# Four states per input and scan instruction, a two-bank PSUM ring, and a reordered tile and prologue in a Mamba cross-attention block with a ternary FFN

## Chip, cores and metric

The kernel runs on one NeuronCore of one Trainium2 chip. The metric is device time of one execution in microseconds (us). A profiled execution gives the trace: the busy spans of TensorE (PE; PEld is its weight load), VectorE (DVE), ScalarE (ACT) and GpSimd (POOL), and the DMA traffic. SyncE (SP) only issues transfers. Each engine runs its own instructions strictly in order and waits on semaphores.

## What is computed

Input `x` is 4 x 512 x 512. A gated state-space (Mamba) block over the context is added to it, then a gated feed-forward net with ternary weights and 8-bit activations. Cut to what matters:

```python
x1    = in_proj_w @ ctx                       # 512 channels, 512 times
u     = silu(causal_conv4(x1) + conv_b)
dt_lo, Bm, Cm = split(x_proj_w @ u)           # 16, 16 and 16 rows
delta = softplus(dt_proj_w @ dt_lo + dt_proj_b)
# 16 states per channel, over time l:
state[l] = state[l-1] * exp(delta[l] * A) + (delta[l] * u[l]) * Bm[l]
y[l]     = sum_n state[l, n] * Cm[l, n]
x  = x + tanh(g_xattn) * (y + D * u) * silu(layernorm(x))
# FFN on rows of x, weights w1, w2, w3 ternarised by mean(|w|), rows quantised to 8 bits:
h  = silu(bitlinear(ln(x), w1, g1)) * bitlinear(ln(x), w2, g2)
x  = x + tanh(g_ffn) * bitlinear(h, w3, g3)
```

## The kernel before

The scan is cut into 16 tiles `k` (4 batches times 4 groups `et` of 128 channels) of 4 steps `q` each, so 64 steps `s = 4k + q`. In a step the 128 partitions hold 32 channels times 4 groups of states, and a partition runs 4 states one after the other along the free axis, 4 x 512 elements. One step is a pipeline over all engines:

- PE spreads `delta*u` of 32 channels over the partitions into the PSUM bank `du_ps` (`bcast_du(s)`, L1484). It waits until all input products of step s-1 have read the bank.
- ACT writes `dA`, the exponentials, four instructions a step (`exps(s)`, L874), two buffers.
- DVE multiplies `du_ps` by B into `dbu_ps` (`add_input(s, half)`, L1129) and scans (`scan(s, half)`, L1138) into `hb`. `dbu_ps` has two banks, so a step is two pairs of input and scan, two states each.
- POOL multiplies `hb` by C (`times_c(s)`, L668). For the last step of a tile with k >= 4 it does so in halves (L663), each of which waits for its own half of the scan.
- PE sums the states into `y_ps` (`sum_states(p)`, L1497, steps 2p and 2p+1 together).

Around the scan the same tile also carries the feed-forward net of earlier rows: row tile `f = k - 4` is normalised, quantised (`quant_scales`, `dequant_scales`) and multiplied by w1 and w2 (`gate_up`, eight PE jobs in step q = 3), and hidden tile `g = k - 5` goes through POOL products (`times_up` L632, `h_gain` L625), DVE maxima (`hidden_max` L1277), `hidden_rms` on POOL (L637, L639), `hidden_scales` on DVE (L1296 to L1298), `quant_hidden` on ACT, transposes and `down` on PE (L1606) and `output` on DVE (L1269). `gated_y(k-1)` (L1260) makes the gated output of the tile before; PE transposes it (`yzT`, L1580) and `add_scan(k-1)` (L1165) adds it to x1.

The order in each engine is written out by hand in one loop over k and q per engine. The relevant pieces: on DVE a step is `add_input(s,0)`, `scan(s,0)`, `add_input(s,1)`, then the tile's other work, `scan(s,1)`; in q = 1 that other work is the two `hidden_max`, `row_bias` and `gated_y`, and `hidden_scales` and `add_scan` come behind `scan(s,1)`. On POOL q = 0 is `times_c(4k-1)`, `times_up` twice, `row_rstd`, `h_gain` twice, and q = 1 is `times_c(4k)`, `hidden_rms`, `mul_du`, `mul_gains`, `hidden_deq`.

All other PE results (projections, convolutions, transposes, gate and up, down) go through a ring of four PSUM banks (`ring`, `NB = 4`). `ring_order()` writes down the order of all jobs; `take(job)` makes PE wait until the job NB places earlier has been read out (`freed_by`). `keep_clock` puts matmuls whose result is not used ahead of some jobs (`FILL`, L1569). When the scan ends (`TAIL`, rows 12 to 15 of the feed-forward net), only that net is left.

In the first 20 steps the weights pass twice through three buffers: ACT sums absolute values (L1034, `abs_chunks`), after step 6 DVE makes the scales (`weight_scales`, L1231), then from step 7 POOL makes one chunk a step ternary (L700), PE transposes it and ACT takes the sign (L1013). B and C of a batch are written to DRAM and read back spread over partitions (`store_bc`, `load_b`, `load_c`, L445 to L463) on SP's queue. `z_row_stats` (L1096) are the layer norm statistics of the gate.

## Times and profile before

| what | value |
|---|---|
| three runs | 718.72, 718.19, 714.82 us; median 718.19 |
| the profiled execution | 720.12 us, of which the span from first to last instruction is 718.1 us |
| DVE busy | 607.9 us (85%) |
| POOL busy | 548.3 us (76%) |
| ACT busy | 558.4 us (78%) |
| PE busy | 619.6 us (86%), in which matmuls of `keep_clock` count too |
| TensorE clock granted, mean | 0.909 |

The busy share of an engine is a mean over stages. The stages are: prologue to 40 us, tiles 0 to 4 with the weights (40 to 224 us), tiles 5 to 15 (224 to 639 us), tail (639 to 718 us). A timeline row gives the start, the time in us, engine, line, operation, output and inputs, and in brackets how long the engine sat idle before it and who ended that.

### The profile page before, as it was taken

The numbers are of one execution on the slowest core, as the hardware profiler recorded it, in microseconds if no ns is written. First come the engines' busy times: TensorE is split into PE (matmuls) and PEld (weight loads), VectorE is DVE, ScalarE is ACT, GpSimd is POOL, SyncE is SP. The second block draws the span as 40 slices with busy tenths as digits, with TensorE's granted clock in tenths as the row PEclk, the third lists the DMA queues.
The fourth block names the chain that finished last, engine by engine and source line by source line (L and its number), as shares of the span: only waits on it lengthen the run. The fifth ranks groups of instructions, "written<-read, shape, count | busy, mean of one in ns | idle before, by whom it ended". The sixth has DMA issues, their size and how long they took to land.

```text
span 718.1 us, 8217 instructions
## 1 busy us (share of the span) xinstructions
PE 619.6 (86%) x2538; PEld 248.4 (35%) x2538; DVE 607.9 (85%) x620; ACT 558.4 (78%) x805; POOL 548.3 (76%) x316
## 2 busy tenths in 40 slices
PE   6736765999869999999989999998897979796997
PEld 3311221544343333334333434332333323233443
DVE  2979959899967899987989899999999989877665
ACT  3647885689679997896879997989698969557873
POOL 2055549987598989897889999999899897967732
PEclk9865887999879999989999999999897979798999
DMA  8599873548922122233411212154111111000000
GB/s 220 168 257 330 287 269 91 165 148 231 297 86 74 44 59 74 59 81 83 93 28 53 52 47 56 46 120 102 49 55 45 45 44 45 15 16 0 16 31 29
DMA packets 40570, 72.01 MB, mean 100 GB/s; under 512 B 10912, under 2 KB 13472, under 8 KB 38352
## 3 DMA queue, kind: packets, MB, share of 16 engines
q1 hardware_dynamic: 37312, 62.07, 30.7%
q10 hardware_dynamic: 3216, 9.44, 3.9%
q8 instruction: 20, 0.33, 0.2%
q14 instruction: 22, 0.18, 0.1%
HBM read 50.51 MB, written 4.46 MB: 77 GB/s over the span
## 4 chain that ended last, share of the span: by engine, by line
PE 44%; DVE 17%; POOL 16%; issue 7%; DMA 7%; ACT 6%; SPq 2%; DVEq 0%; POOLq 0%; ACTq 0%
PE ring L1519 13%; DVE hb L1138 8%; PE y_ps L1497 7%; PE ring L1606 6%; POOL hb L668 6%; DVE dbu_ps L1129 5%; PE du_ps L1484 4%; POOL up_sb L625 4%; PE ring L1569 3%; POOL h L632 3%; DMA dl_rep<-delta 3%; DMA bc_rep<-bc_scratch 2%; PE ring L1446 2%; PE ring L1465 2%; PE ring L1456 2%
## 5 line engine op out<-in xcount | busy, mean ns | idle before, releaser
L1138 DVE TENSOR_TENSOR_SCAN hb<-dA,dbu_ps 128x1024 f32<-128x1024 f32 x128 | 292.4, 2284 | 13.5 <-ACT dA L874 4.6
L668 POOL TENSOR_TENSOR hb<-hb,bc_rep 128x2048 f32<-128x2048 f32 x52 | 235.8, 4537 | 46.7 <-DVE hb L1138 38.8
L874 ACT ACTIVATE dA<-dl_rep,a_neg 128x511 f32<-128x511 f32 x252 | 160.9, 714 | 18.9 <-DMA dl_rep<-delta 18.7
L1129 DVE TENSOR_TENSOR dbu_ps<-du_ps,bc_rep 128x1024 f32<-128x1024 f32 x128 | 157.6, 1231 | 18.5 <-PE du_ps L1484 8.2
L1497 PE MATMUL y_ps<-hb,sel_s 128*32 128x512 f32 x512 | 125.7, 636 | 2.2 <-POOL hb L668 2.2
L1484 PE MATMUL du_ps<-du,sel_q 32*128 32x512 f32 x128 | 79.9, 706 | 46.9 <-DVE dbu_ps L1129 46.5
L632 POOL TENSOR_TENSOR h<-h,up_sb 128x1024 f32<-128x1024 f32 x24 | 56.5, 2353 | 19.8 <-ACT up_sb L892 19.3
L1606 PE MATMUL ring<-w3T,hT 128*128 128x512 fp8e4 x256 | 61.5, 387 | 1.5 <-ACT hT L959 1.1
L663 POOL TENSOR_TENSOR hb<-hb,bc_rep 128x1024 f32<-128x1024 f32 x22 | 51.8, 2357 | 11.9 <-DVE hb L1138 11.6
L1497 PEld LDWEIGHTS y_ps<-hb,sel_s 128*32 128x32 f32 x512 | 28.5, 116 | 87.2 <-issue 81.5
L625 POOL TENSOR_TENSOR up_sb<-h,g3b 128x1024 f32<-128x1024 f32 x24 | 56.4, 2373 | 0.1
L1519 PE MATMUL ring<-w1T,a12T 128*128 128x512 fp8e4 x208 | 54.7, 386 | 1.9 <-ACT a12T L936 1.1
L1519 PE MATMUL ring<-w2T,a12T 128*128 128x512 fp8e4 x208 | 54.4, 384 | 0.0
L929 ACT ACTIVATE up_sb<-up_sb,h_sc 128x1024 f32<-128x1024 f32 x31 | 33.9, 1140 | 25.6 <-DVE h_sc L1298 25.6
L1569 PE MATMUL ring<-w1T,a12T 128*128 128x512 fp8e4 x178 | 48.6, 416 | 0.0
L1484 PEld LDWEIGHTS du_ps<-du,sel_q 32*128 32x128 f32 x128 | 20.5, 199 | 77.0 <-issue 76.5
L884 ACT ACTIVATE h<-ring,deq 128x512 f32<-128x512 f32 x48 | 32.7, 682 | 12.1 <-PE ring L1519 11.9
L1277 DVE TENSOR_REDUCE h_max<-up_sb 128x1 f32<-128x1024 f32 x32 | 38.1, 1210 | 1.8 <-POOL up_sb L625 1.8
L892 ACT ACTIVATE up_sb<-ring,deq 128x512 f32<-128x512 f32 x48 | 32.9, 685 | 7.3 <-PE ring L1519 7.3
L1465 PE MATMUL ring<-u,diag_w 128*128 128x512 f32 (+3 forms) x80 | 38.4, 626 | 0.0
L1446 PE MATMUL ring<-ctxT,w_inT 128*128 128x512 f32 x64 | 36.3, 708 | 2.3 <-ACT ctxT L779 2.3
L959 ACT ACTIVATE hT<-ring 128x1024 bf16<-128x1024 f16 x27 | 26.4, 1018 | 14.3 <-PE ring L1561 13.8
(174 smaller groups left out, 950.6 us busy)
## 6 DMA issues: line engine op xcount, KB each, us to landing
dl_rep<-delta SPq DMA_DIRECT2D x252, 64.0 KB, 2.0
bc_rep<-bc_scratch SPq DMA_DIRECT2D x32, 256.0 KB, 5.2
h<-in_L_ffn_w_dram SPq DMA_DIRECT2D x5, 1024.0 KB, 8.5
x<-in_L_ffn_w_dram SPq DMA_DIRECT2D x5, 1024.0 KB, 7.3
up_sb<-in_L_ffn_w_dram SPq DMA_DIRECT2D x5, 1024.0 KB, 7.9
xt<-in_x_dram SPq DMA_DIRECT2D x16, 256.0 KB, 3.1
out_dram<-x SPq DMA_DIRECT2D x16, 256.0 KB, 2.0
h<-in_L_ffn_w_dram ACTq DMA_DIRECT2D x3, 1024.0 KB, 6.1
```

Of the source, the lines that this page charges most:

```text
L625: g.tensor_tensor(gained(ft)[:, half], hidden(ft)[:, half], g3b[:, half], ALU.mult).then_inc(h_mul, 1)
L632: g.tensor_tensor(h[:, half], h[:, half], up_sb[:, half], ALU.mult).then_inc(h_pool, 1)
L668: g.tensor_tensor(hb[:, s % 4, :, :], hb[:, s % 4, :, :], c_rep(s // 16), ALU.mult)\
L874: ins = a.activation(dA[:, s % 2, i, 1:L], dl[:, 1:L], ACT.Exp, scale=a_neg[:, s % 16, i:i + 1])
L1129: v.tensor_tensor(dbu_ps[:, :, :], du_ps[:, :].unsqueeze(1).to_broadcast([P, 2, L]), b_rep(b)[:, 2 * half:2 * half + 2, :], ALU.mult).then ...
L1138: v.tensor_tensor_scan(hb[:, s % 4, 2 * half:2 * half + 2, :].rearrange("p a l -> p (a l)"), dA[:, s % 2, 2 * half:2 * half + 2, :].rearra ...
L1465: ins = mm(dst[:, shift:L], diag_w[:, DC - 1 - shift, :], u[:, m % UB, 0:L - shift], start=(shift == 0), stop=(shift == DC - 1))
L1484: mm(du_ps[:, :], sel_q[rows, :], du[rows, k % 2, :], start=True, stop=True).then_inc(du_bc, 1)
L1497: ins = mm(y_ps[32 * q:32 * q + 32, :], sel_s[:, :], hb[:, s % 4, i, :], start=False, stop=(i == NH - 1))
L1519: ins = mm(dst[:, :], rows_T(ft)[:, m, t, :], w[:, t, 512 * c:512 * (c + 1)], start=(t == 0), stop=(t == ET - 1))
L1569: mm(dst[:, :], rows_T(ft)[:, t % 2, t // 2 % ET, :], w1T[:, t % ET, 0:512], start=True, stop=True)
L1606: ins = mm(dst[:, :], hT[:, t, :], w3T[:, t, :], start=(t == 0), stop=(t == H // P - 1))
```

## The change

`dbu_ps` gets four banks, so one `add_input` and one `scan` do all four states of a step (2048 elements); only steps 0 and 63 stay in halves. The two banks come from the ring, which has `NB = 2` until the tail; from `TAIL_RING` on the four banks of `dbu_ps` are the ring (`TB = 4`). `times_c` is not changed: its halves now both find the whole scan.

On DVE `hidden_max`, `gated_y` and `hidden_scales` stand between input and scan of q = 1, `add_scan` and `quant_scales` between those of q = 2 (in tiles with et = 0 `add_scan` and the row statistics stay behind the scan of q = 1). `row_var` and `row_bias` of tiles with et other than 0 and `dequant_scales` go to POOL (`row_affine`, `dequant_scales`). POOL's q = 0 becomes `times_c`, `times_up` 0, `h_gain` 0, `times_up` 1, `row_affine`, `h_gain` 1, `hidden_rms`. Diagonal tap matrices are made once, four of them, at the start. Convolutions move from tiles with et = 3 to those with et = 0, which may have two. One `keep_clock` is left out in tiles with et 0 or 3.

In the prologue B of batch 0 is spread by four matmuls (`replicate_b`) and copied by DVE (`copy_b`), half of `z_row_stats` goes into steps 1 to 3, the tanh of the gates goes behind the third `silu_u`, the first three weight chunks are loaded ahead of `store_bc`, and later ones by ACT. The gain vector g3 is loaded in step 18 and not 15. Some small tiles share the buffer `hT` or `sel_q`.

```diff
-NB = 4
+NB = 2
+TB = 4
+def early_convs(k):
+    if k < LEARLY or k % ET == ET - 1:
+        return []
+    m = k + AHEAD - (k % ET == 0)
+    return [m] if m < KQ else []
+def late_convs(k):
+    if k < 1 or k % ET == ET - 1:
+        return []
+    if k % ET == 0:
+        m = [k + AHEAD] if k >= LEARLY else [k + AHEAD - 1, k + AHEAD]
+    else:
+        m = [k + AHEAD] if k < LEARLY else []
+    return [i for i in m if i < KQ]
-    first = (0, 0, 2, 4, 7, 10, WCH)
+    first = (0, 2, 4, 6, 8, 10, WCH)
-        dbu_ps = psum("dbu_ps", [P, 2, L])
+        dbu_ps = psum("dbu_ps", [P, NH, L])
...
+            def row_affine(ft):
+                if ft >= 4:
+                    pool.wait_ge(xn_done, ft - 3)
+                pool.wait_ge(row_square, row_sums(ft))
+                col = fsc[:, ft % 4, :]
+                link(g.tensor_scalar(col[:, 0:1], fmv[:, ft % 4, 1:2], (1.0 + RMS_EPS) / D, RMS_EPS * LN_EPS,
+                                     ALU.mult, ALU.add))
+                link(g.tensor_tensor(col[:, 1:2], col[:, 0:1], half_neg[:, :], ALU.pow))
+                g.tensor_tensor(col[:, 2:3], fmv[:, ft % 4, 0:1], col[:, 1:2], ALU.mult).then_inc(fbias, 1)
...
                     if q == 0 and gt >= 0:
                         times_up(gt, 0)
+                        h_gain(gt, 0)
                         times_up(gt, 1)
                         if f % ET:
-                            row_rstd(f)
-                        h_gain(gt, 0)
+                            row_affine(f)
                         h_gain(gt, 1)
-                    if q == 2 and k + 1 + AHEAD < KQ:
-                        diag_taps(k + 1 + AHEAD)
+                        hidden_rms(gt)
+                    if q == 2 and f >= 0:
+                        dequant_scales(f)
                     if q == 1:
-                        if gt >= 0:
-                            hidden_rms(gt)
...
-            def scan(s, half):
+            def scan(s, lo=0, hi=NH):
-                dve.wait_ge(exp_done, 2 * s + half + 1)
-                if half == 0 and s >= 4:
+                dve.wait_ge(exp_done, 2 * s + hi // 2)
+                if lo == 0 and s >= 4:
                     dve.wait_ge(sum_done, (s - 4) // 2 + 1)
...
-                                     ALU.mult, ALU.add).then_inc(scan_done, 1)
+                                     ALU.mult, ALU.add).then_inc(scan_done, (hi - lo) // 2)
...
-                    add_input(s, 0)
+                    ends = s in (0, Q * KQ - 1)
+                    if ends:
...
+                    else:
+                        add_input(s)
+                    if k == 0 and q >= 1:
+                        z_row_stats(KQ // 2 + 2 * q - 2)
+                        z_row_stats(KQ // 2 + 2 * q - 1)
...
                     if q == 1:
                         if k == 0:
                             convolve(AHEAD)
+                        if g >= 0:
+                            hidden_max(g, 0)
+                            top = hidden_max(g, 1)
+                        if k >= 1:
+                            gated_y(k - 1)
+                        if g >= 0:
+                            after(top)
+                            hidden_scales(g)
                     if q == 2:
                         if f >= 0 and f % ET == 0:
                             row_bias(f)
-                    scan(s, 0)
-                    add_input(s, 1)
+                        if k >= 1 and et:
+                            add_scan(k - 1)
+                        if f >= 0:
+                            quant_scales(f)
                     if q == 3 and g >= 0:
                         output(g)
...
-                    scan(s, 1)
+                    if ends:
+                        scan(s, 2, 4)
+                    else:
+                        scan(s)
                     if q == 1:
-                        if g >= 0:
-                            after(top)
-                            hidden_scales(g)
-                        if k >= 1:
+                        if k >= 1 and et == 0:
                             add_scan(k - 1)
...
+            def replicate_b(n):
+                dst, done = take(("brep", n))
+                mm(dst[:, :], sel_b()[0:DR + 2 * NS, P * n:P * (n + 1)], xdbl[:, :], start=True, stop=True).then_inc(done, 1)
```

## Rows read from the trace of the kernel before

**Rows 1.** Page: TensorE clock granted, in tenths, in 40 slices of the span.

```profile
PEclk9865887999879999989999999999897979798999
```

**Rows 2.** Instructions of line L1138: shortest, median, longest ns, first and last start.

```profile
L1138 DVE TENSOR_TENSOR_SCAN hb<-dA,dbu_ps x128: 2274/2286/2290, 41.6 to 636.8; 128x1024 f32<-128x1024 f32 x128
```

**Rows 3.** Windows: stretch, PE, PEld, DVE, ACT, POOL busy, clock, DMA.

```profile
437.40:473.80 36.40, 34.26 (x142) 12.31 (x141) 34.33 (x34) 34.23 (x50) 33.08 (x17) 0.97 0.19 53
```

**Rows 4.** Timeline of DVE, from the end of tile 10 into tile 11.

```profile
451.68 2.28 DVE L1138 TENSOR_TENSOR_SCAN hb<-dA,dbu_ps 128x1024 f32<-128x1024 f32 x1
454.06 1.23 DVE L1129 TENSOR_TENSOR dbu_ps<-du_ps,bc_rep 128x1024 f32<-128x1024 f32 x1
455.42 2.29 DVE L1138 TENSOR_TENSOR_SCAN hb<-dA,dbu_ps 128x1024 f32<-128x1024 f32 x1
...
461.47 1.23 DVE L1129 TENSOR_TENSOR dbu_ps<-du_ps,bc_rep 128x1024 f32<-128x1024 f32 x1
...
466.30 2.33 DVE L1277 TENSOR_REDUCE h_max<-up_sb 128x1 f32<-128x1024 f32 x2
...
468.67 0.68 DVE L1260 TENSOR_TENSOR yz<-y_ps,xt 128x512 f32<-128x512 f32 x1
469.27 2.28 DVE L1138 TENSOR_TENSOR_SCAN hb<-dA,dbu_ps 128x1024 f32<-128x1024 f32 x1
472.56 0.21 DVE L1296 TENSOR_SCALAR h_sc<-h_pow,h_max 128x1 f32<-128x1 f32 x1 [1.01 <-POOL h_pow L639]
...
473.14 0.73 DVE L1165 SCALAR_TENSOR_TENSOR x<-ring,gates,x 128x512 f32<-128x512 f32 x1
```

**Rows 5.** Timeline of POOL over the same stretch.

```profile
454.03 2.35 POOL L663 TENSOR_TENSOR hb<-hb,bc_rep 128x1024 f32<-128x1024 f32 x1 [1.03 <-DVE hb L1138]
456.34 2.35 POOL L632 TENSOR_TENSOR h<-h,up_sb 128x1024 f32<-128x1024 f32 x1
459.36 2.34 POOL L632 TENSOR_TENSOR h<-h,up_sb 128x1024 f32<-128x1024 f32 x1 [0.68 <-ACT up_sb L892]
461.66 0.55 POOL L653 TENSOR_TENSOR fsc<-fsc,half_neg 128x1 f32<-128x1 f32 x1
462.18 4.71 POOL L625 TENSOR_TENSOR up_sb<-h,g3b 128x1024 f32<-128x1024 f32 x2
466.86 4.51 POOL L668 TENSOR_TENSOR hb<-hb,bc_rep 128x2048 f32<-128x2048 f32 x1
471.36 0.29 POOL L637 TENSOR_SCALAR h_ss<-h_ss 128x1 f32<-128x1 f32 x1
471.73 0.72 POOL L639 TENSOR_TENSOR h_pow<-h_ss,halves 128x2 f32<-128x2 f32 x1
...
473.65 1.27 POOL L613 TENSOR_TENSOR a<-a,g1b 128x512 f32<-128x512 f32 x1
```

**Rows 6.** Timeline of DVE, prologue to tile 5: five rows of its waits.

```profile
33.12 2.46 DVE L1096 BATCH_NORM_STATS2 zst<-g3b 128x6 f32<-128x512 f32 x4
...
40.22 1.23 DVE L1129 TENSOR_TENSOR dbu_ps<-du_ps,bc_rep 128x1024 f32<-128x1024 f32 x1 [4.22 <-DMA bc_rep<-bc_scratch]
...
102.19 0.17 DVE L1231 TENSOR_REDUCE at<-wsum 128x3 f32<-128x12 f32 x1 [6.02 <-ACT up_sb L1034]
...
205.18 0.21 DVE L1189 TENSOR_SCALAR fsc<-fmv,fsc 128x1 f32<-128x1 f32 x1 [6.32 <-POOL fsc L653]
...
224.07 1.23 DVE L1129 TENSOR_TENSOR dbu_ps<-du_ps,bc_rep 128x1024 f32<-128x1024 f32 x1 [3.79 <-PE du_ps L1484]
```

**Rows 7.** Timeline of POOL in tile 4: its wait for C.

```profile
196.92 4.54 POOL L668 TENSOR_TENSOR hb<-hb,bc_rep 128x2048 f32<-128x2048 f32 x1 [7.93 <-DMA bc_rep<-bc_scratch]
```

**Rows 8.** Timelines of PE and ACT: a convolution, a two-tile softplus, a chunk load's issue.

```profile
429.18 3.69 PE L1465 MATMUL ring<-u,diag_w 128*128 128x512 f32 x8
```

```profile
130.18 0.43 ACTq L1017 DMA_DIRECT2D h<-in_L_ffn_w_dram  x1
...
316.19 1.41 ACT L856 ACTIVATE delta<-ring,dtb_col 128x512 f32<-128x512 f32 x2
```

More of the change, by code:

```diff
@@ L77, in ring_order @@
     jobs += [("inproj", m) for m in range(ET)] + [("xproj", 0), ("dt", 0), ("dt", 1)]
+    jobs += [("brep", n) for n in range(NH)]
     jobs += [("ctxT", 1, 0), ("ctxT", 1, 1), ("inproj", ET)]
@@ L236, in flamingo_block @@
         full = [sem(f"ring_full{j}") for j in range(NB)]
+        tail_full = [sem(f"tail_full{j}") for j in range(TB)]
         pool_seq = sem("pool_seq")
@@ L309, in bank, with filling @@
         def bank(job):
-            return ring[RING[job] % NB]
+            n = RING[job]
+            if n >= TAIL_RING:
+                return dbu_ps[:, (n - TAIL_RING) % TB, :]
+            return ring[n % NB]
+        def filling(job):
+            n = RING[job]
+            if n >= TAIL_RING:
+                return tail_full[(n - TAIL_RING) % TB], (n - TAIL_RING) // TB + 1
+            return full[n % NB], n // NB + 1
         def filled(eng, job):
-            eng.wait_ge(full[RING[job] % NB], RING[job] // NB + 1)
+            eng.wait_ge(*filling(job))
         def freed_by(job):
@@ L505, in _ @@
             load_xt(0)
+            for j in range(WB):
+                load_chunk(j)
             store_bc(0)
[L507 removed]
             bcast_delta(1)
             load_c(0)
[L510 removed]
             for k in range(KQ):
@@ L585, in _ @@
                 g.memset(dA[:, j, :, 0:1], 0.0).then_inc(masks, 1)
-            link(g.memset(sel_s[:, :], 0.0))
-            for lo in range(4):
-                link(g.affine_select(out=sel_s[:, :], in_=sel_s[:, :], compare_op=ALU.not_equal, fill=1.0,
-                                     base=-32 * lo, pattern=[[-1, 32]], channel_multiplier=1))
             for j in range(8):
@@ L916, in _ @@
                 tap(et)
-            for et in range(ET):
+            for et in range(ET - 1):
                 silu_u(et)
+            act.wait_ge(ld_gate, 32)
+            a.activation(gates[:, :], gates[:, :], ACT.Tanh).then_inc(gate_done, 1)
+            silu_u(ET - 1)
             step_sizes(0)
@@ L999, in _ @@
                             quant_hidden(g)
-                        if 1 <= k < KQ - AHEAD and not conv_first(k):
-                            conv_evac(k + AHEAD)
+                        for m in late_convs(k):
+                            conv_evac(m)
                     if q == 2 and f >= 0:
@@ L1111, in _ @@
                 conv_tap(et, 3).then_inc(conv_done, 1)
-            z_row_stats(1)
-            z_row_stats(2)
+            for k in range(KQ // 2):
+                z_row_stats(k)
+            for k in range(KQ // 2):
+                z_row_aggr(k)
             dve.wait_ge(delta_done, 1)
@@ L1633, in _ @@
                         skip_term(k)
-                        if 1 <= k < KQ - AHEAD and not conv_first(k):
-                            convolve(k + AHEAD)
+                        for m in late_convs(k):
+                            convolve(m)
                     if q == 2:
```

246 lines of the change are left out of this document (139 added, 107 removed).

## The prediction

> **What bounds the kernel now.** I read the starts of the scans first. The last half scan starts at 636.8 and takes 2.29 [rows 2], so the scans end at 639.1. Tile 5 starts at 224.07 [rows 6]. Eleven of the sixteen tiles thus take 415.0 us, 37.7 each, and they decide. The windows come next: in the 36.4 us of one such tile DVE is busy 34.33 and POOL 33.08 [rows 3]. Neither is full, so I read the two timelines side by side to see what closes the loop. The last scan of tile 10 ends at 453.96 and POOL's product with C starts at 454.03, after an idle 1.03 [rows 4, 5]. Then POOL works without a pause, but for 0.68 spent on ACT, through both `times_up`, `row_rstd`, both `h_gain`, the next product with C (466.86) and `hidden_rms`, which ends at 472.45 [rows 5]. DVE has idled 1.01 for exactly that, then runs `hidden_scales` [rows 4] and goes on without waiting to the next tile's end. So the period is a loop: 18.5 us on POOL from the last scan to `hidden_scales`, then 17.9 us on DVE. In the first five tiles other waits count: 4.22 for B, 6.02 for the weight sums, 6.32 for a row scale and 3.79 for `du_ps` [rows 6].
>
> **Wide instructions.** A DVE product of 512 elements takes 0.68 and one of 1024 takes 1.23 [rows 4], so the constant part is about 0.13 and 2048 elements take 2.33 (estimate). A scan of one half is 2.29; no row has another size, so the wide one lies between 4.43 (same constant part saved) and 4.57 (none). I take 4.43, since both stream from the same engine. A step now costs 3.68 per half with its gaps (input 454.06, scan 455.42, next step 461.47 with one 0.15 us instruction in it, [rows 4]), 7.26 without that one; it will be 2.33 + 0.13 + 4.43 + 0.05 = 6.94. I take 0.4 saved a step, 1.7 a tile. `row_var`, `row_bias` and `dequant_scales` leave DVE in tiles with et other than 0: 0.5 more. DVE's own work in a tile falls from 35.4 (36.4 less 1.0 idle) to 33.2. If all of it arrived, that alone would be 11 x 2.2 = 24 us.
>
> **The loop after the change, tiles 5 to 15, et not 0.** The whole argument turns on this sum. Zero is the end of the last scan of tile k-1.
> - POOL: `times_c` in two halves, both now behind the whole scan, 2 x 2.33; `times_up` 0, `h_gain` 0, `times_up` 1, `h_gain` 1, 4 x 2.33 (starts are 2.31 to 2.36 apart, [rows 5]); `row_affine`, three one-column instructions: a power like 0.55, two like 0.29, with two links, 1.2 (bounds 1.1 and 1.7, the latter all like the powers, [rows 5]). Together 15.2 to the end of `h_gain` 1.
> - DVE meanwhile has input and scan of q = 0, input of q = 1 and the first maximum: 6.94 + 2.25 + 1.13 = 10.3. It then idles 4.9 us, because the second maximum now stands ahead of the whole scan of q = 1. Before, one and a half steps more of input and scan stood ahead of it.
> - From there DVE runs to the tile's end: maximum 1.13, `gated_y` 0.6, `hidden_scales` 0.58 (472.56 to 473.14), scan 4.49, then q = 2: 2.21 + 0.65 (`add_scan`) + 1.57 (`quant_scales`; 1.2 for its maximum as for `hidden_max`, and four scalar steps) + 4.47, then q = 3: 2.21 + 0.66 (`output`) + 4.43. Together 23.0 [rows 4].
> - Sum 38.2, against 36.4. What leaves the loop is the product with C of q = 0 (4.5), `hidden_rms` (1.1, now beside the second maximum), ACT's 0.68 (hidden by `h_gain` 0), and about 1.1 of DVE's savings. What enters is half of `times_c` (2.3), the rest of `row_affine` (0.65), maximum and `gated_y` (1.7) and the scan of q = 1 (4.5). Nine such tiles: 343.8.
>
> **Tiles with et = 0 (8 and 12).** `add_scan` and the row statistics stay behind the scan of q = 1 and end at about 22.6. `row_rstd`, `row_bias` (25.1), `normalise` on ACT and two gains of 1.27 on POOL [rows 5] follow. Until now a half scan and an input stood between `row_bias` and `quant_scales`; now nothing does, so DVE idles some 3.5. The tile comes to 41.9; two are 83.8.
>
> **The ring of two banks.** `hT` 1 needs the bank of `yzT`, which `add_scan` frees at 24.8; gate 0 needs that of `down`, freed by `output` at 33.7; each later gate or up job waits for the evacuation of the one before its neighbour, so the eight take 0.93 instead of 0.86 each. `bcast_du` behind gate 0 then lands at about 37, before DVE wants it at 38.2, and `times_up` 0 wants its inputs 4.7 after that, so the cover holds by 1 to 2 us. Where it doesn't hold: in tiles 5 and 9 the two step-size jobs fill both banks until ACT's softplus (1.41 for two, behind four exponentials and a table load), then the convolution (3.69) [rows 8], `yzT` and `bcast_du` follow in line on PE, and `du_ps` is ready 2 us late; in tile 7 `x_proj` puts the state sum 1.8 behind. Together 5.8. Bounds for the ring over the eleven tiles: 0, if PE finds the gaps, and 30, if every tile loses 2.7. Tiles 5 to 15 are then 343.8 + 83.8 + 5.8 = 433.4, that is 18.4 more than before.
>
> **Prologue and tiles 0 to 4.** B by matmul: the halves of step 0 and four copies (4 x 0.7, like the 0.68 of `gated_y` [rows 4]) stand on DVE, and `bcast_du(1)` stays behind `in_proj(5)` on PE, so step 1 starts some 0.6 earlier than now and not the 4.22 [rows 6]. Eight row statistics (2.46 for four, [rows 6]) and eight small aggregates (0.1 each, estimate) move from cover into steps 1 to 3: +5.7. Steps 1 to 19 save 19 x 0.4: -7.6. The weight sums: twelve sums at two a step on ACT, begun earlier, cut the 6.02 to about 2.5: -3.5; each load that ACT issues costs it 0.43 [rows 8], nine of them, under DVE's work. From the scales on, POOL's product, first ternary chunk, series, product, and PE's sum keep their length while DVE reaches `gated_y(1)` earlier, so it waits 3.5 more: +3.5. In tile 4 the load of g3 no longer stands ahead of C's in SP's queue, and the input of step 15 is done in one piece, so C lands before POOL's 7.93 of waiting [rows 7]; DVE's 6.32 [rows 6] goes, but `quant_scales` waits 3.6 as in tiles 8 and 12: -2.7. The 3.79 for `du_ps` [rows 6] goes, since a whole step of DVE work now stands ahead of it: -3.8. In tiles 2 and 3 PE and ACT, with two ring banks and twelve chunks of four jobs, take back some of the saving: 0 to +6, taken as +1. Sum -8.0 (range -20 to +5). The four tap matrices in the prologue (POOL, idle then), the moved tanh, and the tail with its four banks of `dbu_ps` I put at nothing. POOL waits in the prologue for the row statistics and ACT for the convolution taps; without that cover it is at most 4 x 1.27, one 512-element product each [rows 5], and one activation of two columns.
>
> **Sum.** 718.1 - 8.0 + 18.4 = 728.5, 1.4% more. The profiled execution took 720.12 with a span of 718.1, and the median of the runs is 718.19, so median and span agree and the forecast is 728.
>
> **A rule weighed.** The Trainium skill, Perfetto Trace Analysis, section Optimizing Scalar/DVE Operations, says that grouping into larger operations helps when the engine is saturated, and that breaking instructions up may let work finish sooner when the engine only causes bubbles elsewhere. By the first half the time would be near rival 1, by the second near the forecast; DVE's idle 1.01 a tile says that it is not quite saturated. Its section Matmul Optimizations wants all eight PSUM banks used for independent jobs, which speaks for rival 2.
>
> **Rival 1, the saving goes through (faster).** If the chain over POOL did not close the loop, the tile would be set by POOL's own work, 33.08 and some 1.0 for what it is given [rows 3, 5], about 34.5, and 38 with et = 0: 386.5 for eleven tiles, 28.5 less than before. With -8.0 that is 682; half of it gives 700. For it: `hidden_rms` and `hidden_scales` are each put earlier, and POOL's first gain hides ACT. Against: 15.2 of POOL must fit beside 10.3 of DVE. It decides where `h_gain` 1 ends before DVE reaches the second maximum.
>
> **Rival 2, the ring binds.** PE starts its gate jobs only when DVE has put out the tile before, and every late `bcast_du` stops DVE. From 2.7 lost a tile on, that is 30 us: 728 + 24 = 752. For it: the granted clock is already 0.7 to 0.9 late in the scans [rows 1], and PE waits more between its jobs. Against: the 1 to 2 us of cover above.
>
> **Rival 3, a wash.** The loop is 38.2, but the early tiles give back 18 to 20: 715 to 718.
>
> **Chances.** Forecast 0.45 (716 to 742), rival 1 0.27 (680 to 712), rival 2 0.18 (738 to 762), rival 3 0.10 (711 to 722). About 0.5% (3.6 us) is what a measurement can tell from no change. Faster: 0.27 + 0.02 + 0.04 = 0.33. Same: 0.07 + 0.05 = 0.12. Slower: 0.55. The likeliest case alone is 716 to 742; the range that leaves out no more than 2 in 10 is 694 to 750.
>
> **What would show it.** Right: in tiles 5 to 15 DVE idles 4 to 5 us before the second maximum, released by POOL's gain; scans at 4.43; periods of 38; tile 8 and 12 at 42 with an idle before `quant_scales`; tile 5 starts near 216. Wrong: if that idle is under 1 us, rival 1; if the longest waits of DVE are for `du_ps`, rival 2; if scans take 4.57, 0.14 a step comes on top.

## Result: 785.7 us, 9.7% slower

Three kinds of numbers follow: run times, profiled spans, and starts of the input of q = 0 of a tile, from which the periods are taken.

| | before | after |
|---|---|---|
| median of the runs | 717.5 us (718.2 in the first three) | 785.7 us (784.6 to 787.7) |
| ratio | 1 | 1.0971, 95% interval 1.0933 to 1.1008 |
| profiled span | 718.1 | 783.0 |
| mean granted clock | 0.909 | 0.876 |
| start of tile 0 | 40.2 | 39.8 |
| tiles 0 to 4 | 183.8 | 215.4 |
| tiles 5 to 15 | 415.0 | 447.6 |
| tail | 79.0 | 80.2 |
| periods, tiles 0 to 4 | 33.6, 40.3, 32.5, 33.6, 43.9 | 43.9, 44.3, 37.5, 40.6, 49.0 |
| periods, tiles 5 to 15 | 38.2, 36.4, 42.1, 38.8, 37.9, 36.4, 36.4, 37.1, 36.8, 37.4, 37.3 | 42.0, 42.9, 39.7, 41.7, 42.8, 38.9, 38.9, 42.5, 41.2, 38.0, 39.0 |

The sign was forecast, the size was not: 728 forecast, 694 to 750 the range. Tile 5 starts at 255.2, where the forecast had 216. First the costliest DVE groups of the changed kernel, shapes apart (line, engine, operation, shapes, count | busy us, mean ns | idle before it and who ended it):

```profile
L1216 DVE TENSOR_TENSOR_SCAN hb<-dA,dbu_ps 128x2048 f32<-128x2048 f32 x62 | 273.8, 4417 | 2.6
L1207 DVE TENSOR_TENSOR dbu_ps<-du_ps,bc_rep 128x2048 f32<-128x2048 f32 x62 | 142.6, 2300 | 51.9 <-PE du_ps L1577 47.1
L1354 DVE TENSOR_REDUCE h_max<-up_sb 128x1 f32<-128x1024 f32 x32 | 38.7, 1214 | 43.6 <-POOL up_sb L664 43.6
L1275 DVE TENSOR_REDUCE am<-a 128x2 f32<-128x1024 f32 x13 | 15.8, 1213 | 17.4 <-POOL a L652 17.4
```

The wide instructions cost what they were put at (4.42 and 2.30), so DVE has less to do. It has more to wait for: 47.1 us before wide inputs, 43.6 before the maxima, 17.4 before the row maxima. The middle one is the wait of the forecast, in its place. Tile 11 on POOL and DVE of the changed kernel (start, us, engine, line, operation, idle before it):

```profile
510.32 2.35 POOL L664 TENSOR_TENSOR up_sb<-h,g3b 128x1024 f32<-128x1024 f32 x1
512.63 2.35 POOL L671 TENSOR_TENSOR h<-h,up_sb 128x1024 f32<-128x1024 f32 x1
...
516.12 2.36 POOL L664 TENSOR_TENSOR up_sb<-h,g3b 128x1024 f32<-128x1024 f32 x1
```

```profile
512.71 1.22 DVE L1354 TENSOR_REDUCE h_max<-up_sb 128x1 f32<-128x1024 f32 x1 [0.28 <-POOL up_sb L664]
518.52 1.22 DVE L1354 TENSOR_REDUCE h_max<-up_sb 128x1 f32<-128x1024 f32 x1 [4.59 <-POOL up_sb L664]
519.65 0.68 DVE L1337 TENSOR_TENSOR yz<-y_ps,xt 128x512 f32<-128x512 f32 x1
...
520.91 4.42 DVE L1216 TENSOR_TENSOR_SCAN hb<-dA,dbu_ps 128x2048 f32<-128x2048 f32 x1
```

Where [rows 4] show 1.01 idle before `hidden_scales`, there is now 4.59 before the second maximum, and the whole scan behind it. Tiles 10 and 11 take 38.9, forecast 38.2. But tiles 5 to 9 take 39.7 to 42.9, and tiles 0 to 4 have grown by 31.6. There the other kind of wait stands: TensorE's waits (engine, output, line <- who ended it: us in total, times, longest) in the changed kernel:

```profile
PE du_ps L1577 <- DVE dbu_ps L1207: 20.6, 5, 8.1
PE ring L1685 <- ACT delta L916: 16.7, 4, 8.0
PE ring L1685 <- DVE yz L1337: 15.3, 4, 5.3
PE ring L1666 <- DVE x L1243: 9.1, 5, 2.5
PE ring L1558 <- ACT delta L916: 9.1, 2, 5.8
PE ring L1515 <- ACT w3T L1076: 8.2, 4, 5.8
PE ring L1674 <- ACT hT L1022: 6.3, 6, 2.2
```

The first is a wait for `du_ps`, which VectorE must read out (46.5 us in 21 waits in the kernel before), and the third is for data; the other five are waits for a bank of the ring. In the kernel before the same view has no wait of the gated transposition or the convolution for the delta and none of a filler; the only waits of the tiles in it that are plainly for a ring bank are two of 0.8. That made the ring the first suspect. Tile 9 shows what such a wait does; TensorE's convolution, VectorE's next input, and two windows (stretch, PE, PEld, DVE, ACT, POOL busy, clock, DMA):

```profile
440.31 5.90 PE L1558 MATMUL ring<-u,diag_w 128*128 128x512 f32 x8 [5.76 <-ACT delta L916]
447.79 2.30 DVE L1207 TENSOR_TENSOR dbu_ps<-du_ps,bc_rep 128x2048 f32<-128x2048 f32 x1 [4.13 <-PE du_ps L1577]
436.50:440.30 3.80, 0.00 (x0) 0.02 (x1) 3.38 (x6) 3.77 (x6) 3.62 (x4) 0.70 0.37 96
440.30:443.00 2.70, 2.69 (x4) 1.15 (x5) 2.70 (x1) 1.73 (x2) 2.70 (x2) 0.50 0.46 132
```

The wait costs twice. TensorE stands 5.76 us, and the granted clock falls from full to 0.50 (1.2 of 2.4 GHz) while it stands. The convolution behind it then takes 5.90 us where the same one takes 3.69 at full clock in this kernel (310.46) and in the kernel before [rows 8]. Tile 5 is alike: 3.31 of standing, 5.76 for the convolution, 4.38 of waiting on VectorE.

### The profile page after: what moved, and what is told of

Same layout as the page of the kernel before. It is cut to its first block, busy times and chain, and to the rows that moved or that the text cites. A ratio compares the mean times of both kernels' runs of the same rounds, so it can differ in the third digit from the quotient of the medians.

```text
span 783.0 us, 8040 instructions
## 1 busy us (share of the span) xinstructions
PE 648.3 (83%) x2506; PEld 250.4 (32%) x2506; DVE 592.7 (76%) x458; ACT 560.9 (72%) x804; POOL 549.9 (70%) x341
## 4 chain that ended last, share of the span: by engine, by line
PE 23%; DVE 17%; POOL 11%; issue 11%; ACT 7%; DMA 0%; DVEq 0%; ACTq 0%; POOLq 0%
DVE hb L1216 12%; POOL h L671 5%; PE ring L1612 4%; POOL hb L723 4%; PE dbu_ps L1612 3%; PE y_ps L1590 3%; ACT dA L934 3%; PE dbu_ps L1711 2%; PE du_ps L1577 2%; POOL up_sb L664 2%; PE ring L1558 1%; PE ring L1674 1%; PE ring L1711 1%; DVE am L1275 1%; DVE x L1243 1%
## 5 line engine op out<-in xcount | busy, mean ns | idle before, releaser
L1216 DVE TENSOR_TENSOR_SCAN hb<-dA,dbu_ps 128x2048 f32<-128x2048 f32 (+1 forms) x66 | 283.0, 4287 | 2.9
L1207 DVE TENSOR_TENSOR dbu_ps<-du_ps,bc_rep 128x2048 f32<-128x2048 f32 (+1 forms) x66 | 147.5, 2234 | 55.0 <-PE du_ps L1577 50.1
L1590 PE MATMUL y_ps<-hb,sel_q 128*32 128x512 f32 x512 | 128.6, 648 | 5.4 <-POOL hb L728 5.4
L1577 PE MATMUL du_ps<-du,sel_q 32*128 32x512 f32 x128 | 84.0, 740 | 20.6 <-DVE dbu_ps L1207 20.6
L1354 DVE TENSOR_REDUCE h_max<-up_sb 128x1 f32<-128x1024 f32 x32 | 38.7, 1214 | 43.6 <-POOL up_sb L664 43.6
L1590 PEld LDWEIGHTS y_ps<-hb,sel_q 128*32 128x32 f32 x512 | 28.9, 118 | 93.3 <-issue 82.4
L1612 PE MATMUL ring<-w1T,a12T 128*128 128x512 fp8e4 x192 | 49.3, 378 | 4.6 <-DVE x L1346 3.2
L1612 PE MATMUL ring<-w2T,a12T 128*128 128x512 fp8e4 x192 | 49.5, 380 | 0.0
L1558 PE MATMUL ring<-u,diag_w 128*128 128x512 f32 (+3 forms) x80 | 41.7, 673 | 9.1 <-ACT delta L916 9.1
L1022 ACT ACTIVATE hT<-ring 128x1024 bf16<-128x1024 f16 x22 | 21.8, 1019 | 32.2 <-PE ring L1666 32.2
L1674 PE MATMUL ring<-w1T,a12T 128*128 128x512 fp8e4 x138 | 38.9, 423 | 6.3 <-ACT hT L1022 6.3
L1711 PE MATMUL ring<-w3T,hT 128*128 128x512 fp8e4 x176 | 42.5, 385 | 0.0
L1685 PE MATMUL ring<-ident,yz 128*128 128x128 f32 x64 | 12.9, 337 | 32.6 <-ACT delta L916 16.7
```

Source lines behind the costliest of these rows:

```text
L1207: v.tensor_tensor(dbu_ps[:, lo:hi, :], du_ps[:, :].unsqueeze(1).to_broadcast([P, hi - lo, L]), b_rep(b)[:, lo:hi, :], ALU.mult).then_inc(d ...
L1216: v.tensor_tensor_scan(hb[:, s % 4, lo:hi, :].rearrange("p a l -> p (a l)"), dA[:, s % 2, lo:hi, :].rearrange("p a l -> p (a l)"), dbu_ps[ ...
L1558: ins = mm(dst[:, shift:L], diag_w[:, m % ET, DC - 1 - shift, :], u[:, m % UB, 0:L - shift], start=(shift == 0), stop=(shift == DC - 1))
L1577: mm(du_ps[:, :], sel_q[rows, :], du[rows, k % 2, :], start=True, stop=True).then_inc(du_bc, 1)
L1590: ins = mm(y_ps[32 * q:32 * q + 32, :], sel_q[:, 0:32], hb[:, s % 4, i, :], start=False, stop=(i == NH - 1))
L1612: ins = mm(dst[:, :], rows_T(ft)[:, m, t, :], w[:, t, 512 * c:512 * (c + 1)], start=(t == 0), stop=(t == ET - 1))
```

## Experiments

Each is compared with the kernel before on the same chip. "Periods" are read as above. The times of 738.9, 783.0, 779.3, 781.5 and 901.6 us are single runs, so differences of a few us from them are not shown to be real.

### The ring alone

```diff
-NB = 4
+NB = 2      # in the kernel before; NB = 3 in the second
```

> The kernel before with one number changed: the ring has two banks and not four; input and scan stay in halves, all orders as before. Ring theory (the 32 us lost in tiles 0 to 4 come from PE standing in line behind a bank that ACT or DVE has not read out): tiles 1 to 4 together grow from 150.3 us by 20 us or more, DVE waits for du_ps for 40 us or more (8.2 before), total 750 to 790 us. Width theory (the loss comes from whole steps of input and scan and from what was moved in the prologue): tiles 1 to 4 grow by under 8 us, total 715 to 735 us.

> The kernel before with a ring of three banks. Ring theory: one more bank breaks most of the line behind the two step-size jobs, so the loss is a third of that with two banks or less, total 722 to 745 us. If the loss falls in proportion (half of the two-bank loss), it is the number of waits and not the one line behind the softplus. Width theory: 716 to 722 us.

With two banks the kernel before took **796.2 us, ratio 1.106 (1.096 to 1.117)**. This one constant costs more than the whole change. By stages against before: start of tile 0 +2.9, tiles 0 to 4 +28.1 (33.6, 48.0, 37.3, 46.5, 46.5), tiles 5 to 15 +30.1 (445.1), tail +15.1. The ring theory held, though the time lies above its 750 to 790 and the waits for `du_ps` came to 38.5 and not 40. With three banks it took 738.9 (before 719.3): about a quarter of the loss. So the price rises steeply with the last bank taken. The changed kernel has four banks in its tail, and its tile 0 doesn't start later, so 58 of these 76 can bear on it. That these 58 carry over in full is not shown: no run gives the changed kernel four banks, which its version in halves would allow.

Tile 1 with two banks shows the longest piece, TensorE and then ScalarE and VectorE:

```profile
88.57 1.98 PE L1474 MATMUL ring<-xdbl,w_dtT 16*128 16x512 f32 x4
97.96 1.11 PE L1580 MATMUL ring<-ident,yz 128*128 128x128 f32 x4 [7.41 <-ACT delta L856]
```

```profile
91.46 1.91 ACT L1034 ACTIVATE h<-h 128x2048 f32<-128x2048 f32 x1 [2.25 <-DMA h<-in_L_ffn_w_dram]
93.28 0.19 ACT L1034 ACTIVATION_READ_ACCUMULATOR h<-h 128x1 f32 x1
93.37 2.54 ACT L874 ACTIVATE dA<-dl_rep,a_neg 128x511 f32<-128x511 f32 x4
95.92 1.28 ACT L844 ACT_TABLE_LOAD   x1
97.22 1.26 ACT L856 ACTIVATE delta<-ring,dtb_col 128x512 f32<-128x512 f32 x2
```

```profile
99.11 0.75 DVE L1165 SCALAR_TENSOR_TENSOR x<-ring,gates,x 128x512 f32<-128x512 f32 x1 [7.34 <-PE ring L1580]
101.11 1.23 DVE L1129 TENSOR_TENSOR dbu_ps<-du_ps,bc_rep 128x1024 f32<-128x1024 f32 x1 [1.25 <-PE du_ps L1484]
```

Two step-size products fill both banks. ScalarE empties them only after a weight sum, four exponentials and a table load. TensorE stands 7.41 us (granted clock 0.50 in the 3.1 us after it), and behind it the gated transposition and the broadcast that VectorE wants next.

### Which jobs hold whom

The kernel before with its four banks given out as two pairs, so that the jobs of one pair never wait for the other.

```diff
+PAIR_B = ("gate", "up")             # then with "wT", "wsum"; then ("gate", "up", "dt"); then all of them
-    return ring[RING[job] % NB]
+    return ring[BANK[RING[job]]]    # the two banks of its pair in turn, waiting for the last but one job of the pair
```

> The kernel before with its four ring banks, given out in two pairs: the gate and up products have two banks to themselves, every other job the other two. Ring of two over the whole (the earlier run) cost 77 us: 28 in tiles 0 to 4, 30 in tiles 5 to 15, 15 in the tail. Theory A, the bank is lost at the seam: with two banks the input projection of the next tile waits until ScalarE has emptied the last up product, and the state broadcast stands behind it on TensorE; the gate products among themselves never need more than two. Then tiles 5 to 15 come back to 37.7 to 38.5 each and the tail to 80, tiles 0 to 4 stay near 205 (the weight transposes still share two banks with the rest), total 735 to 750. Theory B, the loss is between neighbours of the same kind (a gate product waits for the gate product two before it, a transposition for the one two before it): tiles 5 to 15 stay at 39.5 or more, total 775 to 790.

> As the run with the gate and up products in a pair of their own, with the weight transposes in that pair too. Theory A (jobs of one kind need two banks, what costs is the wait across kinds): tiles 0 to 4 fall from about 205 to 185 to 192, total 718 to 730. Theory B (the weight transposes move in lock-step with ScalarE's signs, four jobs to a chunk, and that binds with two banks whoever else has them): tiles 0 to 4 stay at 200 or more, total as the run before it.

> The kernel before with four ring banks in two pairs: gate, up and step-size (dt) products in one, all other jobs in the other. In the run with only the gate and up products apart, the two dt products of every second tile filled both general banks, and the gated transposition behind them waited for ScalarE's softplus: TensorE waited 17.2 us in 4 waits for the delta (longest 7.5), VectorE 21.3 us for the transposed product. Theory A, that is the largest single piece of the two-bank loss: those waits go, tile 1 falls from 47.4 to 40 to 42 and tile 3 from 46.5 to 37 to 40, tiles 5, 7 and 9 by 1 to 4 each, total 755 to 765. Theory B, behind that wait stands another of the same length (the convolution's ScalarE evacuation or the state broadcast): the wait changes its name and the total stays at 775 to 783.

> As the run with the dt products apart, with the weight transposes in that pair too. Putting these apart beside the gates alone took 4.0 us off tile 3 and nothing off the others. Theory A: both pieces add, tile 3 near 35, total 748 to 760. Theory B: dt products and weight transposes now share a pair and hold each other (tile 3 has both), no gain over the run before it, or a loss to 770.

| pair of their own | time | tiles 0 to 4 | tiles 5 to 15 | tail |
|---|---|---|---|---|
| none (ring of two) | 796.2 | 211.9 | 445.1 | 94.1 |
| gate, up | 781.9 | 211.2 | 444.1 | 83.8 |
| gate, up, weights | 778.8 | 207.3 | 444.6 | 83.8 |
| gate, up, step sizes | 757.3 | 193.8 | 433.3 | 84.9 |
| gate, up, step sizes, weights | 759.9 | 197.4 | 433.3 | 85.3 |

Gate and up products apart help the tail alone (10 us); theory A of the first run, a loss at the seam between tiles, fell. The weight transposes apart from the general jobs gave 4.0 in tile 3 (46.5 to 42.5), far from the 185 to 192 of theory A for tiles 0 to 4, and took 3.6 back in tiles 0 to 4 when they shared with the step sizes. TensorE's waits for ScalarE's signs stay in a pair of their own (10.7, 3.0 and 2.9 us for the three matrices against 7.8, 2.7 and 2.6 with the ring of two), which fits a lock-step with ScalarE. The step-size products apart gave 24.6 us (27 by the profiled spans), within the 755 to 765 expected: tile 1 goes from 47.4 to 38.7, tile 3 from 46.5 to 39.2, tiles 5 and 9 by 3.6 and 4.0, but tile 7 grew from 41.8 to 43.3 where a gain was expected. TensorE goes straight on in tile 1:

```profile
88.08 1.98 PE L1482 MATMUL ring<-xdbl,w_dtT 16*128 16x512 f32 x4
89.99 0.66 PE L1588 MATMUL ring<-ident,yz 128*128 128x128 f32 x4
```

So nearly half of the two-bank loss in the tiles (28 of 58 us) is this one kind of job, whose products stay longest in their banks. The other 28 us against the kernel before were not taken apart by a run, but the trace of the ring of two shows one more piece. In tile 6 two jobs of context transposes stand between `down` and the state sum, and the first needs the bank of `down`, which only `output` on VectorE frees:

```profile
333.73 1.94 PE L1422 MATMUL ring<-ident,h 128*128 128x128 f32 x8 [5.23 <-DVE x L1269]
342.94 1.23 DVE L1129 TENSOR_TENSOR dbu_ps<-du_ps,bc_rep 128x1024 f32<-128x1024 f32 x1 [7.17 <-PE du_ps L1484]
```

Tile 6 takes 45.7 and not 36.4, the largest loss of any of the eleven tiles. Again the clock falls with the wait, to 0.50, and the transposes take 1.94 where they took 1.04 before. With the step sizes apart the 5.2 of waiting stays and the tile takes 43.7. The changed kernel has the same wait at 2.56, with 4.20 on VectorE behind it, and its tile 6 takes 42.9.

The lock-step of the gate products, which the forecast had, is next to nothing in these three: from the first gate product to the broadcast behind the last up product it is 9.0 us before (450.16 to 459.12), 9.0 with the gates in a pair and 9.1 in the changed kernel, because the broadcast waited for VectorE anyway. What does show is gate 0 behind `output`, in tile 10 of the ring of two:

```profile
503.89 1.02 PE L1519 MATMUL ring<-w1T,a12T 128*128 128x512 fp8e4 x4 [1.67 <-DVE x L1269]
```

### The width alone

The changed kernel with each input and scan cut in halves again, everything else as changed.

```diff
-                        add_input(s)
+                        add_input(s, 0, 2)
+                        scan(s, 0, 2)
+                        add_input(s, 2, 4)
...
-                        scan(s)
+                        scan(s, 2, 4)
```

> The changed kernel, but every step is again input and scan of two states, twice, with the tile's other work ahead of the second scan as before the change; ring, order of the other engines and prologue as changed. If whole steps are what costs: in tiles 10, 11, 14 and 15 the product with C of the first half starts a half scan earlier and only half a scan stands behind the second maximum, so the period falls from 38.9 to about 36.5 us and the total to 755 to 765 us. If the order of the other work costs and not the width: the period stays at 38 to 39 and the time grows by what the halves cost DVE, 0.4 us a step, total 785 to 805 us. Tiles 0 to 4 stay within 8 us of the 215 us of the changed kernel if the ring is what costs there.

783.0 us, against 785.7 (784.6 to 787.7) with whole steps. This lies between the two expectations, 2 us below that of the order; tiles 0 to 4 take 216.5, within 8 of 215 as the ring theory had it. Waits for `du_ps` rise from 50.1 to 80.5 us, and the time doesn't grow. What a wide step saves is real in its instructions and buys nothing of the whole: the halves are no slower. The two banks given for it cost 58 us or so in the kernel before; this run leaves the ring at two banks and so can't show their price in the changed one.

### The idle before the second maximum, and the broadcast

```diff
-                            hidden_max(g, 0)
-                            top = hidden_max(g, 1)
...                                              # now behind the scan of q = 1, with hidden_scales
+                            hidden_max(g, 0)
+                            after(hidden_max(g, 1))
```

> The changed kernel with one move on DVE: in q = 1 the two hidden maxima and the hidden scales stand behind the whole scan and not ahead of it. Loop theory (my prediction's step): POOL's 15 us now lie beside one and a half steps plus a scan (14.3 us), so the 3.3 to 4.6 us of idle before the second maximum go, the period of tiles 10, 11 and 14 falls from 38.9 to 34.5 to 35.5 us, and the total by 30 to 40 us, to 745 to 755 us. Rival (POOL's own work or du_ps sets the period once the idle is gone): the period stays above 37 us and the total above 770 us, with the idle of DVE now ahead of its inputs.

787.6 us, ratio 1.094 (1.083 to 1.106): nothing, where the loop theory had 745 to 755. The rival came true. The waits of the 38.2 us loop are gone, and others of the same size have come. DVE's waits in this run:

```profile
DVE dbu_ps L1207 <- PE du_ps L1575: 50.0, 24, 7.0
DVE yz L1337 <- PE y_ps L1588: 44.2, 15, 6.7
```

The second loop runs over TensorE, same run:

```profile
509.04 1.03 PE L1610 MATMUL ring<-w2T,a12T 128*128 128x512 fp8e4 x4
510.00 1.12 PE L1575 MATMUL du_ps<-du,sel_q 32*128 32x512 f32 x2
511.05 3.63 PE L1547 MATMUL ring<-u,w_xT 128*48 128x512 f32 x8
514.61 3.63 PE L1588 MATMUL y_ps<-hb,sel_q 128*32 128x512 f32 x16
```

The state sum that `gated_y` needs stands behind eight gate and up products, the broadcast and `x_proj`. It ends at 518.2 and `gated_y` starts at 518.29, after an idle of 4.31, 13.6 us into tile 11; in the changed kernel the second maximum started 15.4 us into it. Tiles 10 and 11 take 38.6 and 38.9. The forecast saw one loop, and by these rows there were two of nearly one length. It put `gated_y` on the path only as DVE time.

Two more, with TensorE's broadcast for q = 2 put ahead of the step-size products and the gated transposition, alone and with the maxima behind the scan:

```diff
+                        bcast_du(s + 1)        # q == 1, ahead of dt_proj
...
-                        bcast_du(s + 1)
```

> The changed kernel with one move on PE: in q = 1 bcast_du(s+1) stands ahead of the step-size jobs, the convolution and yzT and not behind them. If the line behind the softplus (both ring banks full, PE waits for ACT) is what makes DVE wait for du_ps: most of DVE's 50.1 us of waiting for du_ps that falls in odd tiles goes, 20 to 28 us, and the total falls to 755 to 770 us. If the other loops (POOL to the second maximum, PE to the state sum) only take the time over: the waits for du_ps shrink but the total falls by under 10 us, to 774 to 785 us.

> The changed kernel with both moves, du_ps first on PE and maxima behind the scan on DVE. If each move alone only handed the time to the other loop, the two together gain more than the sum of both: total 740 to 765 us. If the third chain, from the gate jobs over x_proj or in_proj to the state sum and gated_y, sets the period by itself, the tiles 10, 11 and 14 stay at 38 to 39 us and the total at 765 to 785 us, with DVE waiting for y_ps 40 us or more.

779.3 and 781.5. In the first the waits for `du_ps` fall from 50.1 to 28.9 us, and 6 us of these 21 arrive, in tiles 0 to 4 (215.4 to 209.8; tiles 5 to 15 stay at 447.8). With both moves they are 32.6, and `gated_y` waits 44.3 for the state sum, as the third chain of the expectation had it; the two moves don't add. Removing any one wait here hands most of it to the next engine.

### TensorE's fillers

```diff
-FILL = (4, 10, 4)
+FILL = (0, 0, 0)
```

> The changed kernel without the 18 filler products per tile that TensorE does to hold its clock (4 ahead of a gated transposition, 10 ahead of the hidden transpositions, 4 ahead of the down projection); nothing of the result hangs on them. Theory A, TensorE's own chain (gate and up products, state broadcast, x_proj and in_proj, state sum) now sets the end: the fillers are in that chain, and without them tiles 5 to 15 fall by 1 to 3 us each if the clock holds, total 755 to 775. If the clock falls with them, the chain's products run longer and it comes out slower, 790 to 830. Theory B, TensorE waits at banks and the fillers lie in those waits: no change in the tiles at the same clock, 780 to 788.

784.9 us at a mean granted clock of 0.854 (0.876 with fillers). Neither the fillers nor the 0.02 of clock that they hold is on the path: TensorE is 83% busy in the changed kernel by the page, and 138 of its 2506 products can go for nothing.

### The kernel before with one part of the change

```diff
                         times_up(gt, 0)
-                        times_up(gt, 1)
-                        row_rstd(...)
-                        h_gain(gt, 0)
+                        h_gain(gt, 0)
+                        times_up(gt, 1)
+                        row_rstd(...)
                         h_gain(gt, 1)
+                        hidden_rms(gt)         # ahead of times_c of q = 1
```

> The kernel before (four ring banks, halves) with POOL's order of the change alone: h_gain 0 between the two times_up, hidden_rms directly behind h_gain 1 and ahead of the product with C of q = 0. Loop theory: 4.5 us leave the chain from the last scan to hidden_scales, DVE's idle of 1.0 to 1.6 us before it goes, the period of tiles 10, 11 and 14 falls from 36.4, 36.4 and 37.4 to 35.3 to 36, and the total by 8 to 14 us, to 704 to 710 us. Rival: PE's line (gate jobs, du_ps, state sum) has the same length and takes over, so the period stays above 36 us and the total falls by under 5 us.

> The kernel before with the second gain moved ahead on GpSimd, once more, as the base that the others stand beside: 706 to 714.

> The kernel before with the second gain moved ahead on GpSimd, and without TensorE's 18 filler products per tile; nothing of the result hangs on them. In the changed kernel leaving them out changed nothing in time (784.9 against 785.7) while the granted clock fell from 0.876 to 0.854. Theory A, TensorE sets no end here and its slower products stay covered: 703 to 712, clock 0.88 to 0.90. Theory B, the fillers hold the clock for the broadcast and the gate products, which VectorE waits for: 715 to 730.

Only GpSimd's order of the change, on four banks and half steps: **710.2 us, ratio 0.9925 (0.9883 to 0.9967)**, a small gain clear of the noise. The same kernel once more, beside other runs: 705.6 us against 718.1, ratio 0.9834 (0.9762 to 0.9906). Tile 11 on DVE in the first, to be laid beside [rows 4]:

```profile
456.20 2.33 DVE L1276 TENSOR_REDUCE h_max<-up_sb 128x1 f32<-128x1024 f32 x2
458.45 0.20 DVE L1188 TENSOR_SCALAR fsc<-fmv,fsc 128x1 f32<-128x1 f32 x1
458.57 0.68 DVE L1259 TENSOR_TENSOR yz<-y_ps,xt 128x512 f32<-128x512 f32 x1
459.17 2.27 DVE L1137 TENSOR_TENSOR_SCAN hb<-dA,dbu_ps 128x1024 f32<-128x1024 f32 x1
461.37 0.18 DVE L1295 TENSOR_SCALAR h_sc<-h_pow,h_max 128x1 f32<-128x1 f32 x1
```

The idle of 1.01 is gone. Tiles 10 and 11 take 35.4 and 36.1 here, 35.4 and 35.3 in the second, and not 36.4; tile 14 stays at 37.5 (37.4 before), where 35.3 to 36 was expected. So the reading of the loop before was right for tiles 10 and 11, and the change held its own remedy. Without fillers the same kernel took 706.0 (ratio 0.9808, 0.9715 to 0.9902) at a clock of 0.886: no different from 705.6 with them. These are the fastest versions of the study, below both kernels. That 710.2 and 705.6 are one kernel shows that results of different batches may differ by some 5 us.

### Four states wide without the ring's banks

The kernel before with four ring banks, whole steps, the input product written to SBUF (`hb`) and scanned in place, GpSimd's order and the maxima behind the scan.

```diff
-        dbu_ps = psum("dbu_ps", [P, 2, L])
...
-                v.tensor_tensor(dbu_ps[:, :, :], ...
+                v.tensor_tensor(hb[:, s % 4, :, :], ...
...
-                v.tensor_tensor_scan(hb[...], dA[...], dbu_ps[...], 0.0, ...
+                v.tensor_tensor_scan(row, dA[...], row, 0.0, ...
```

> The kernel before with whole steps and all four ring banks: the input product is written to the scan's own output buffer hb in SBUF and the scan works in place, so no bank is taken from the ring; POOL's order as in the changed kernel, the hidden maxima behind the scan of q = 1. If the ring is the whole cost of the change and an operand in SBUF costs the scan nothing, tiles 10 and 11 take 34.5 to 36 us and the total is 685 to 705 us. Rival: the Trainium skill, SBUF — State Buffer, says that a DVE instruction with two SBUF inputs and a GpSimd instruction that reads SBUF exclude each other for their whole length. By that rule DVE's scans (18 us a tile) no longer run beside POOL's products (33 us a tile): the period is 50 us or more and the total over 850 us, with scans or POOL products that look stretched.

901.6 us, where the rival had over 850. The scan now reads two tensors of SBUF, and GpSimd's products read SBUF too:

```profile
559.06 5.89 DVE L1134 TENSOR_TENSOR_SCAN hb<-dA,hb 128x2048 f32<-128x2048 f32 x1
...
567.26 4.43 DVE L1134 TENSOR_TENSOR_SCAN hb<-dA,hb 128x2048 f32<-128x2048 f32 x1
```

```profile
556.13 4.54 POOL L667 TENSOR_TENSOR hb<-hb,bc_rep 128x2048 f32<-128x2048 f32 x1 [4.36 <-DVE hb L1134]
565.03 8.80 POOL L662 TENSOR_TENSOR hb<-hb,bc_rep 128x1024 f32<-128x1024 f32 x2 [4.36 <-DVE hb L1134]
```

GpSimd's product ends at 560.67. The scan that started at 559.06 ends 4.28 after that. So it is throughout: 52 of the 64 scans start while a GpSimd instruction is under way and end 4.24 to 4.31 after it. The two half products span 8.80 where one takes some 2.35 [rows 5], and a scan of 4.43 (567.26) lies inside them. The rows fit one of the two standing still until the other is done. So the product has to sit in PSUM, and two more banks for it could here only come from the ring.

## Why the prediction was right or wrong

- **Which wait closes the loop before**: right. GpSimd's order alone removes the 1.01 and takes 1.0 off tile 10 and 0.3 or 1.1 off tile 11.
- **Wide instructions**: right, 4.42 and 2.30 against 4.43 and 2.33.
- **The loop of 38.2**: right in place, size and tiles 10 and 11 (38.9; idle 4.59 + 0.28 against 4.9), and incomplete: a second loop over TensorE's state sum has nearly the same length, so taking the first away gave nothing.
- **Tiles with et = 0**: tile 12 takes 42.5 (forecast 41.9) with 3.57 idle before the row maxima (forecast 3.5). Tile 8 takes 41.7.
- **The ring, tiles 5 to 15**: the step that failed. It was put at 5.8 with bounds of 0 and 30. The changed kernel has 447.6 where the forecast without its ring term has 427.6: 20.0. The ring alone on the kernel before measured 30.1, at the upper bound. The value was taken from an argued cover of 1 to 2 us for one broadcast, and from 2 us in two tiles for the step-size jobs. The runs showed that the step-size jobs cost 11 us in these eleven tiles (444.1 to 433.3) and not 4. In the changed kernel the miss sits where TensorE stands at a bank: tiles 5, 6, 9 and 13 are 3.8, 4.7, 4.6 and 3.0 above the forecast's 38.2, the other seven 3.9 together above theirs. The line behind the softplus in tiles 5 and 9 was named, but with the convolution at 3.69; it took 5.76 and 5.90, because the clock fell while TensorE stood, and VectorE waited 4.4 and 4.1 and not 2. The context transposes of tile 6 had no term at all.
- **The ring, tiles 0 to 4**: the larger miss. It was put at +1 (0 to +6) and measured 28.1 alone, on the kernel before. How much of it the changed kernel pays is not measured. Here step-size products wait behind weight sums, and twelve chunks of four transposes pass through the same two banks; [rows 8] gave the softplus behind four exponentials and a table load, and in tile 1 a weight sum with its own DMA wait stood ahead of that as well. No term had it. The weight sums themselves were to make VectorE wait 2.5; it waited 8.69 (6.02 before), since ScalarE stood 7.95 for a convolution ahead of the last two sums.
- **Prologue**: -8.0 forecast for the prologue and the early tiles, +31.2 measured (-0.4 and +31.6). Beside the ring, step 1's input starts 14.2 us after step 0's; before it was 7.4. The forecast had step 1 0.6 earlier. Of the 6.8, 2.7 are two copies of B and their waits within step 0, and the rest is a broadcast. This is read from the trace and no run isolates it. The input of step 1 in the changed kernel, and TensorE ahead of it:

```profile
53.99 2.30 DVE L1207 TENSOR_TENSOR dbu_ps<-du_ps,bc_rep 128x2048 f32<-128x2048 f32 x1 [4.08 <-PE du_ps L1577]
```

```profile
39.70 3.78 PE L1638 MATMUL ring<-xdbl,a12T 48*128 48x512 f32 x4
43.41 1.97 PE L1515 MATMUL ring<-ident,a 128*128 128x128 f32 x8
46.06 6.78 PE L1539 MATMUL ring<-ctxT,w_inT 128*128 128x512 f32 x8 [0.69 <-ACT ctxT L839]
52.77 1.12 PE L1577 MATMUL du_ps<-du,sel_q 32*128 32x512 f32 x2
```

  `bcast_du(1)` stands behind the added B products, eight transposes and two projections. The two take 6.78 where one takes 1.98 later at full clock (77.94); the granted clock is 0.50 from 36 to 46 us and 0.54 over the projections, and 0.80 and then 1.00 between 40 and 46 us in the kernel before. Some 2.8 of the 4.08 is then the clock (estimate, from 6.78 less twice 1.98). The 4.22 of waiting for B [rows 6] became 4.08 of waiting for the broadcast one step later. With the row statistics in steps 1 to 3 (1.27 + 1.28 + 2.46 + 0.63 = 5.6, forecast 5.7) this takes tile 0 from 33.6 to 43.9 (6.8 and 5.6, less what the wide steps save). The ring has little part in it: TensorE's only wait between the B products and the broadcast is 0.69, for data, and with the ring of two alone tile 0 keeps its 33.6.
- **Tile 4**: the 6.32 and 3.79 of [rows 6] were to go. In their place stand 10.22 before the row maxima and 7.09 for `du_ps`. Why the gains are that late there was not tested.
- **Rivals**: rival 2 named the cause, that the ring binds, and the sign of it to look for, `du_ps` as DVE's longest wait in total (50.1). Its price of 2.7 a tile in eleven tiles was right for the ring alone (30.1) and above the 20.0 of the changed kernel; what put its 752 too low was that it had no price at all for tiles 0 to 4. It gave the clock, 0.7 to 0.9 late in the scans, as a sign that speaks for it, and put no price on it either. Rival 1 and rival 3 fell.

By stages the account closes: 728.5 forecast, +14.2 in tiles 5 to 15, +39.6 in tiles 0 to 4 (27 the ring beyond the 1 forecast, if its price on the kernel before carries over, 7.4 step 1's start; some 5 stay unassigned, about the size of the miss at the weight sums, 6.2), +1.2 tail and -0.4 start give 783.1, the span. That the sum closes doesn't show its parts.

The Trainium skill, Perfetto Trace Analysis, section Matmul Optimizations, wants all eight PSUM banks in use. All eight are in use in both kernels, so the rule as it stands doesn't tell them apart. The runs do: what counts here is the number of independent jobs that may be open at once.

## What to carry to other kernels

Before banks are taken from a ring that serves several engines, list for each job when its product is read out, not how long that takes, and look for two slow readers in a row: in a ring of two they stall everything queued behind, and the clock that TensorE loses in the wait makes the queue longer. The cheapest test is to change the ring's depth alone and leave the rest; here it would have settled the change at once (4, 3 and 2 banks: 718, 739, 796 us). A price that the trace of before can't show, with bounds of 0 and 30, belongs nearer the middle than at the end that an argued cover suggests, and it must be asked for in every stage.

## What the hardware showed

- VectorE's scan with two SBUF inputs and GpSimd's products exclude each other for a whole instruction: 8.81 us is the longest scan and 5.74 the mean where 4.42 is the time alone. In the changed kernel, with one input in PSUM, scans took 4.42 throughout beside the same products. The Trainium skill, SBUF — State Buffer, section "SBUF: two separate sides", describes such an exclusive lock between a VectorE instruction with two SBUF inputs and a GpSimd instruction that reads SBUF; the trace agrees.
- Two scans of 1024 elements take 2 x 2.284 us and one of 2048 takes 4.417: 0.15 us saved by the wide one.
- Leaving out the fillers lowered the mean granted clock by 0.02 in the changed kernel and by 0.03 in the kernel before with GpSimd's order, and no time moved. But where TensorE has stood at a bank and VectorE waits for what is queued behind, the clock is on the path: after 5.76 us of standing a convolution took 5.90 us at a granted clock of 0.62, and 3.69 at full clock.
